# A 512-value bias row spread by TensorE, W's first block transposed after the tables, and three filler products ahead of B

## The reference, cut to what matters

```
w = weights[subjects];  b = bias[subjects]          # (128, 64, 64), (128, 64)
x = x + einsum('bct,bcd->bdt', x, w) + b[:, :, None]            # layer 0
H = einsum('btd,od->bto', x, W)                                 # W: 512 x 512
xa = einsum('btd,brd->btr', x, A[adapter_idx])                  # rank 16
delta = einsum('btr,bor->bto', xa, Bm[adapter_idx]) * scalings[adapter_idx]
x = x + H + delta                                               # layer 1
```

## Time and profile before

| | us |
|---|---|
| median of 3 runs | 241.46 |
| lowest, highest | 241.38, 241.91 |
| the profiled execution | 241.36 |
| its span | 239.6 |

### The profile page before, as it was taken

One profiled execution on the slowest core, in us unless ns is written; L12 is line 12 of the kernel. 1 busy time (PEld: TensorE's weight loads), 2 busy tenths in 40 slices (PEclk: granted clock), 3 DMA queues, 4 the chain that ended last, 5 costly groups with the idle time before them and its releaser, 6 DMA issues.

```text
span 239.6 us, 9653 instructions
## 1 busy us (share of the span) xinstructions
PE 229.4 (96%) x2900; PEld 187.7 (78%) x2901; DVE 149.2 (62%) x259; ACT 107.9 (45%) x185; POOL 79.6 (33%) x277
## 2 busy tenths in 40 slices
PE   1899999999999999999999999999999999999992
PEld 1787878888887888888888888888788888888761
DVE  6799848873358636875258835875448754425762
ACT  3184663543436363562436354454435434344441
POOL 4467771700077610610056730525135131000000
PEclk9999999999999999999999999999999999999998
DMA  5956455736565474645555574645646364562233
GB/s 132 279 169 193 141 176 156 198 94 176 148 197 141 120 213 131 201 108 192 134 154 163 147 215 109 192 115 160 172 135 191 109 200 110 155 178 63 83 78 90
DMA packets 23723, 36.64 MB, mean 153 GB/s; under 512 B 6162, under 2 KB 6162, under 8 KB 23698
## 3 DMA queue, kind: packets, MB, share of 16 engines
q1 hardware_dynamic: 16480, 26.10, 40.0%
q10 hardware_dynamic: 7218, 10.23, 13.7%
HBM read 19.53 MB, written 16.78 MB: 152 GB/s over the span
## 4 chain that ended last, share of the span: by engine, by line
PE 89%; DVE 2%; DMA 2%; ACTq 2%; issue 1%; ACT 1%; DVEq 0%
PE ps L883 69%; PE ps L843 14%; PE ps L819 3%; DMA o_ring<-in_L_cond_W_dram 2%; PE ps L764 1%; ACTq L693 1%; PE ps L775 1%; DVE o_ring L554 1%; ACT x_hi L658 1%; ACT m_f L681 1%; DVE x_lo L534 0%; PE ps L813 0%; DVE last_parts L539 0%; PE ps L871 0%; DVE o_ring L549 0%
## 5 line engine op out<-in xcount | busy, mean ns | idle before, releaser
L883 PE MATMUL ps<-m_hi,x_hi 128*128 x244 | 97.0, 398 | 0.0
L883 PE MATMUL ps<-m_hi,x_lo 128*128 x244 | 95.1, 390 | 0.0
L883 PE MATMUL ps<-m_lo,x_hi 128*128 x244 | 95.1, 390 | 0.0
L534 DVE TENSOR_TENSOR x_lo<-x,x_hi 128x512 fp32r<-128x512 f32 x64 | 44.7, 698 | 62.8 <-ACT x_hi L658 62.4
L374 POOL COPY p_pair<-p_all 64x64 f32 x128 | 42.8, 335 | 113.8 <-DVE x L526 96.9
L658 ACT ACTIVATE x_hi<-x 128x512 fp32r<-128x512 f32 x64 | 40.4, 632 | 56.0 <-ACT o_ring L671 30.9
L671 ACT ACTIVATE o_ring<-ps 128x512 f32<-128x512 f32 x60 | 35.9, 598 | 52.1 <-PE ps L883 50.7
L883 PEld LDWEIGHTS ps<-m_hi,x_hi 128*128 128x128 f32 x244 | 45.8, 188 | 10.7 <-issue 0.4
L883 PEld LDWEIGHTS ps<-m_hi,x_lo 128*128 128x128 f32 x244 | 45.8, 188 | 9.7
L883 PEld LDWEIGHTS ps<-m_lo,x_hi 128*128 128x128 f32 x244 | 45.8, 188 | 9.0
L526 DVE TENSOR_TENSOR x<-ps,bias_pair 128x512 f32<-128x512 f32 x64 | 43.6, 685 | 11.1 <-PE ps L843 10.1
(11 more groups left out here) (102 smaller groups left out, 82.4 us busy)
## 6 DMA issues: line engine op xcount, KB each, us to landing
x_ring<-in_x_dram SPq DMA_DIRECT2D x122, 128.0 KB, 2.7
out_dram<-o_ring ACTq DMA_DIRECT2D x64, 128.0 KB, 2.6
out_dram<-o_ring SPq DMA_DIRECT2D x64, 128.0 KB, 2.3
a_f<-in_L_cond_A_dram SPq DMA_DIRECT2D x8, 128.0 KB, 2.7
x_ring<-in_x_dram ACTq DMA_DIRECT2D x6, 128.0 KB, 3.4
o_ring<-in_L_cond_W_dram SPq DMA_DIRECT2D x2, 256.0 KB, 4.7
o_ring<-in_L_cond_W_dram ACTq DMA_DIRECT2D x2, 256.0 KB, 5.8
b_nat<-in_L_cond_Bm_dram ACTq DMA_DIRECT2D x1, 256.0 KB, 3.7
```

The lines of the kernel that those rows point to most:

```text
L534: nc.vector.tensor_tensor(x1_lo[:, u % HELD], x1[:, u % 2], x1_hi[:, u % HELD], ALU.subtract).then_inc(x1_lo_ready, 1)
L883: mm = nc.tensor.matmul(ps[:, 2 + u % 2, :], part, m_tile(m, k, c), start=(c == 0 and part is hi and m is m_hi), stop=(c == TC - 1 and par ...
```

## The change

1. Bias. The 256 KB DMA on ACT's queue is removed. SP loads the row to one partition (`bias_row`, 2 KB) as its second DMA, ahead of W's first block. TensorE spreads it: four products of a row of ones with 128 columns of `bias_row` each, into PSUM bank 5, three of them ahead of the order product and the fourth after the scalings. ACT copies the bank to `bias_all`.
2. W's first block is turned after the tables rather than between the scalings and the tables, and only when bank 5 is free (`bias_ready`).
3. After it stand three products of the bfloat16 identity with two copies of itself (256 columns), into the bank that B is turned into next, `keep_busy(b_bank(0), 3)`; then B is turned, and W's third block only after B.
4. x loads of the first quad: SP now loads both halves of pair 3 (five loads), ACT three.
5. `wt`: ACT copies chunks 0 to 2, DVE chunk 3, and DVE splits A before its copy.
6. POOL zeroes the second half of `a_parts` after pair 3, not at the start.
7. At the end, if pair 63 is computed apart, ACT copies its even half's lower part (`copy_last_low`) before it stores the odd item of pair 62; afterwards only the odd half's is left.

```diff
@@ block.sync
+            sp.dma_start(bias_row[:], bias.rearrange("s d -> (s d)").rearrange("(a n) -> a n", a=1)).then_inc(bias_in, 16)
             sp.dma_start(w_nat[:, 0, :], W[0:P, :]).then_inc(w_in[0], 16)
...
-            b = words(sp, regs[:5], batch[0:1, 2:7], B - 1)
+            b = words(sp, regs[:6], batch[0:1, 2:8], B - 1)
             for i in range(1, XR):
                 load_half(sp, i, 0, b[2 * i - 2], x_first[i])
+            load_half(sp, XR - 1, 1, b[2 * XR - 3], x_first[XR - 1])
             load_a(1, 1)
@@ block.gpsimd
+                if n is None and j == HEAD - 1:
+                    pool.wait_ge(pair_ready, j * 4 + 4)
+                    nc.gpsimd.memset(a_parts[0:GR, 1, :].bitcast(F32), 0.0).then_inc(rows_zeroed, 1)
+                    pool.wait_ge(rows_zeroed, 2)
@@ block.vector
-            dve.wait_ge(wt_turned, 1)
-            nc.vector.tensor_copy(wt[:, 0, :], ps[:, FIRST, :]).then_inc(wt_copied_too, 1)
             a_split(0, 0)
+            dve.wait_ge(wt_turned, TC)
+            nc.vector.tensor_copy(wt[:, TC - 1, :], ps[:, FIRST + TC - 1, :]).then_inc(wt_copied_too, 1)
@@ block.scalar
-            act.dma_start(bias_all[:], bias.rearrange("s d -> (s d)").rearrange("(a n) -> a n", a=1)
-                          .to_broadcast([P, S * C]).rearrange("p (s d) -> p s d", s=S)).then_inc(bias_in, 16)
...
-                    for half in range(2):
-                        act.wait_ge(low_done[half][i], 1)
-                        nc.scalar.activation(low[0:C, half], ps[C:2 * C, 2 + 2 * half + u % 2, :],
-                                             ACT.Copy).then_inc(low_ready, 1)
+                    for half in range(2) if j < PAIRS - 1 else (1,):
+                        copy_low_half(j, u, half)
...
+            def copy_last_low(j, u):
+                act.wait_ge(out_ready, j)
+                with act.If_ne(last_places[MIXED - 1][0], last_places[MIXED - 1][1]):
+                    copy_low_half(j, u, 0)
...
+            act.wait_ge(bias_spread, 1)
+            nc.scalar.activation(bias_all[:].rearrange("p s d -> p (s d)"), ps[:, 5, :], ACT.Copy).then_inc(bias_ready, 1)
             act.wait_ge(batches_ready, 1)
-            b = words(act, last_regs, batch[0:1, 0:2 * XR], B - 1)
-            for i in range(XR):
-                load_half(act, i, 1, b[2 * i + 1], x_first[i])
+            b = words(act, last_regs[:5], batch[0:1, 1:6], B - 1)
+            for i in range(XR - 1):
+                load_half(act, i, 1, b[2 * i], x_first[i])
...
                     copy_low(j, u)
+                    if j == PAIRS - 2:
+                        copy_last_low(j + 1, u + 1)
                     store_odd(j, u, last_batches[2 * n_of_mixed(j) + 1])
@@ block.tensor
+            def spread_bias(part):
+                cols = slice(part * P, part * P + P)
+                return nc.tensor.matmul(ps[:, 5, cols], ones[0:1, :], bias_row[:, cols], start=True, stop=True)
+            def keep_busy(bank, times):
+                for _ in range(times):
+                    nc.tensor.matmul(ps[:, bank, 0:2 * P], ident_b[:], ident_b[:].unsqueeze(1).to_broadcast([P, 2, P]),
+                                     start=True, stop=True)
+            pe.wait_ge(bias_in, 16)
+            for part in range(TC - 1):
+                spread_bias(part)
...
+            pe.wait_ge(bias_ready, 1)
+            pe.wait_ge(w_in[0], 16)
+            for c in range(TC):
+                turn_w(0, c)
+            pe.wait_ge(scal_ready, 1)
+            keep_busy(b_bank(0), 3)
+            turn_b(0)
```

More of the change, by code:

```diff
@@ L92, in cond_residual_layers @@
         scal_row = sb("scal_row", [1, K])
+        bias_row = sb("bias_row", [1, S * C])
         neg = sb("neg", [P, 2])
@@ L149, in cond_residual_layers @@
         bias_in = sem("bias_in")
+        bias_spread = sem("bias_spread")
+        bias_ready = sem("bias_ready")
         bnat_in = sem("bnat_in")
@@ L333, in _ @@
             pool.wait_ge(consts, 6)
-            for half in range(2):
-                nc.gpsimd.memset(a_parts[GR - GR * half:P - GR * half, half, :].bitcast(F32), 0.0).then_inc(rows_zeroed, 1)
-                pool.wait_ge(rows_zeroed, half + 1)
+            nc.gpsimd.memset(a_parts[GR:P, 0, :].bitcast(F32), 0.0).then_inc(rows_zeroed, 1)
+            pool.wait_ge(rows_zeroed, 1)
             pool.wait_ge(bnat_in, 16)
@@ L382, in step @@
                 if isinstance(j, int) and j == 0:
-                    pool.wait_ge(bias_in, 16)
+                    pool.wait_ge(bias_ready, 1)
                 for half in range(2):
@@ L558, in _ @@
             dve.wait_ge(zeroed, 3)
-            dve.wait_ge(rows_zeroed, 2)
+            dve.wait_ge(rows_zeroed, 1)
             dve.wait_ge(w0_in, 16)
@@ L579, in _ @@
             x1_add(2, 2)
+            dve.wait_ge(rows_zeroed, 2)
             a_split(1, 1)
@@ L671, in copy_out, with copy_low_half @@
                 nc.scalar.activation(o_ring[:, u % OR, :], ps[:, 2 + u % 2, :], ACT.Copy).then_inc(out_ready, 1)
+            def copy_low_half(j, u, half):
+                i = n_of_mixed(j)
+                act.wait_ge(low_done[half][i], 1)
+                nc.scalar.activation(low[0:C, half], ps[C:2 * C, 2 + 2 * half + u % 2, :],
+                                     ACT.Copy).then_inc(low_ready, 1)
             def copy_low(j, u):
@@ L704, in _ @@
             nc.scalar.activation(scal_all[:], ps[:, 6, 0:K], ACT.Copy).then_inc(scal_ready, 1)
+            act.wait_ge(bias_spread, 1)
+            nc.scalar.activation(bias_all[:].rearrange("p s d -> p (s d)"), ps[:, 5, :], ACT.Copy).then_inc(bias_ready, 1)
             act.wait_ge(batches_ready, 1)
-            b = words(act, last_regs, batch[0:1, 0:2 * XR], B - 1)
-            for i in range(XR):
-                load_half(act, i, 1, b[2 * i + 1], x_first[i])
+            b = words(act, last_regs[:5], batch[0:1, 1:6], B - 1)
+            for i in range(XR - 1):
+                load_half(act, i, 1, b[2 * i], x_first[i])
             a_round(0, 0)
+            copy_wt(0)
             copy_wt(1)
             copy_wt(2)
-            copy_wt(3)
             last_batches = words(act, last_regs, batch[0:1, B - 2 * MIXED:B], B - 1)
@@ L783, in _ @@
             nc.tensor.matmul(ps[:, 6, 0:K], ones[0:1, :], scal_row[:], start=True, stop=True).then_inc(scal_spread, 1)
-            pe.wait_ge(w_in[0], 16)
-            for c in range(TC):
-                turn_w(0, c)
+            spread_bias(TC - 1).then_inc(bias_spread, 1)
             pe.wait_ge(place_ready, 1)
@@ L797, in _ @@
                 turn_w(2, c)
-            turn_b(0)
             for c in range(TC):
@@ L807, in m_product_first @@
             def m_product_first(chunk):
-                if chunk == 0:
+                if chunk == TC - 1:
                     pe.wait_ge(wt_copied_too, 1)
                 else:
-                    pe.wait_ge(wt_copied, chunk)
+                    pe.wait_ge(wt_copied, chunk + 1)
                 nc.tensor.matmul(ps[:, FIRST + chunk, :], a_parts[:, 0, chunk * P:chunk * P + P], b_parts[:],
```

## The result

| | before | changed |
|---|---|---|
| median of 6 runs each, us | 241.51 (241.38 to 241.91) | 242.87 (242.30 to 243.70) |
| profiled execution, us | 241.36 | 242.30 |
| its span, us | 239.6 | 240.6 |

The ratio is 1.0045 (1.0029 to 1.0061): slower, by 1.1 us, where 1.0 faster was forecast, and outside the range.

The account below looks back on a forecast made before the run. TensorE was taken as the bound except at the start (SP's x loads for the second quad) and the end (ACT's copies, DVE's sums). 241.36 - 0.2 (start) - 0.77 (end) = 240.4 us; range 239.7 to 241.1.

Parts of the forecast that it names:

- The end: Last pairs: with one ACT copy moved ahead, pair 63's odd sum starts earlier, 0.77 us gained (bounds 0.5 to 0.86).
- Between them TensorE works through a fixed queue, so a start that is x earlier reaches the last pairs as x: Between start and end: TensorE is the bound, so any gain at the start arrives whole at the last pairs.
- B's transposes or the third block's are 110 apart rather than 213: Start, TensorE: sign expected in the profile if the clock rises early, transposes 110 ns apart.
- the 12.4 worked out for the slow pace: Start, TensorE: end of the transposes' queue in us at the old pace, against 11.93 before.
- Rival 3: Start, TensorE: clock rises no earlier than now since transposes don't count; queue ends at 12.4, time 240.7; 8%.
- All x loads may be issued 0.25 earlier: Start: the batch product, freed from W's transposes, can start at 6.47 instead of 6.72, moving x loads up 0.25 us.
- I take 3.0 and a start at 21.7: Second quad: SP's last x load lands 3.0 us after issue, not 3.6; quad starts at 21.7, 0.2 gained.
- rival 2: Start: SP's queue eats the gain, second quad starts at 22.3, 0.4 late; time 241.0; 13%.
- Each 0: Start: moving POOL's zeroing and giving `wt` to another engine each change nothing, between 0 and 0.1 us.
- Rival 5: TensorE: slower, as the clock rises early and falls again; 4%.
- The chance of 0.05 for slower: Whole kernel: probability given to the change being slower, beside 0.81 for faster and 0.14 for same.

Follow-up runs that it names:

- kernel 1: Kernel before with part 7 alone (pair 63's even copy ahead of pair 62's odd store): 240.81 us, ratio 0.996.
- kernel 3: Changed kernel plus twelve one-element products at the start of TensorE's program (about 48 instructions): 241.80 us, ratio 1.001.
- kernel 5: Changed kernel with its part 4 undone (x loads split as before): 242.51 us, ratio 1.0048.
- 9: Changed kernel with part 4 undone and twelve one-element products at the start of TensorE's program: 241.33 us, ratio 0.9989.
- 2: Kernel before plus six one-element products at the start of TensorE's program (about 24 instructions): 242.71 us, ratio 1.0039.
- 12: Kernel before plus three one-element products at the start of TensorE's program (12 instructions): 241.60 us, ratio 0.9996.
- 4: Changed kernel without part 3's three products of the identity with itself: 242.23 us, ratio 1.0019.
- 10: Changed kernel with part 4 undone, twelve one-element products at the start, and without part 3's three identity products: 241.19 us, ratio 0.9984.
- kernel 7: Kernel 1 plus four products of the identity, all 128 rows, in the gaps of TensorE's start: 240.77 us, ratio 0.9966.
- kernel 6: Kernel before with parts 4 to 7 of the change alone: 241.27 us, ratio 0.9981.
- 11: Kernel 1 plus twelve one-element products at the start of TensorE's program (48 instructions): 241.20 us, ratio 1.0002.

## Why the prediction was wrong, step by step

**The end: right.** -0.77 forecast, 0.72 in the profile, 0.86 by kernel 1's median.

**"Between them TensorE works through a fixed queue, so a start that is x earlier reaches the last pairs as x": this step failed, and it is the largest part of the miss.** Without the wait the change is still no gain: kernel 3 stands level with before (1.001, 0.9988 to 1.0032). The order of the work is fixed, but not the time at which the engine has its instructions. Parts 1 to 3 add 11 products to TensorE, and with them the place at which it stops for its next instructions came to stand early in layer 1 of pair 2. The price by medians is +1.07 (changed less 3), +1.18 (5 less 9) and +1.04 (2 less before, late x included). (Changed and 3 were timed in different sets; by their ratios the first is 0.85.) What is shown: the wait depends on the count of instructions ahead, no semaphore releases it, and it can be made and removed without touching any data. It also goes with the packet of q8 in every profile (the table above): late where the packet went out within the dense run, gone where it went out ahead of it. So 48 more instructions cost no wait: the packet then goes out 2 to 4 us sooner, while layer 1 still runs at 0.23 a product. In before it goes out late too, but the place stands later in the twelve: by the steps of kernels 2 to 12 at about the eleventh product, near 26.5 (an estimate), and 23.93 and 1.56 are 25.5. The DMA view of the changed kernel, 23.6 to 23.7, and of kernel 3, 20.6 to 20.7:

```profile
q8 instruction: 1, 0.02, 75.8%
...
q8 instruction: 1, 0.02, 92.6%
```

What is still inferred is that TensorE stands for these very instructions: no view names what a packet holds or which instruction was missing. What asks for the packet at that moment is not shown either.

**"B's transposes or the third block's are 110 apart rather than 213": failed.** The prediction let the clock rise early. In the changed kernel's profile it rose at about 12.4, and the queue of transposes ended at 12.50, which is the 12.4 worked out for the slow pace. But the early rise does come in others: of the six profiles that have the start of parts 1 to 3, four rise between 9.6 and 10.6 (4, 5, 9, 10), two at 12.1 to 12.4 (3 and changed). Kernel 7, with full products in the gaps, rises at 11.3, and none of the other seven before 11.9, the latest (6) at about 13.7. One profile of each can't say more than that an early rise came with added work only, and can't be counted on, as TensorE's program of the changed kernel alone gives 12.4 and 9.6. Rival 3 named the late rise, but for a reason (transposes don't count) that kernels 4, 5 and 10 contradict: there neighbouring transposes go from 421 ns to 273 or 274. The error cost little: where the rise was early the second quad started at 22.88 and 21.97, no sooner than before.

**"All x loads may be issued 0.25 earlier": half right; a term was put at nothing.** SP's first went out at 7.32. ACT's did not move (8.51). The copy of the bias (6.36 to 6.96) is not the reason: kernel 5 has it and issues its first x load at 8.01, kernel 6 has not and issues at 8.65. It is ACT's fetch of the batch words into registers. Part 4 has it fetch five words from the second on; before and kernel 5 fetch eight from the first on. The fetch in the changed kernel, then in 5 (min/median/max ns):

```profile
L249 ACTq TENSOR_LOAD <-batch x1: 1327/1327/1327, 6.9 to 6.9; - x1
...
L249 ACTq TENSOR_LOAD <-batch x1: 761/761/761, 6.9 to 6.9; - x1
```

It takes 1.32 in kernel 6 too, and 0.76 in before. Why fewer words take longer is not shown.

**"I take 3.0 and a start at 21.7": failed.** The start was 22.25, the number of rival 2 (22.3), but not by its path. SP's last load went out at 17.80, not 18.2, and landed at 21.73, 3.9 later. The chain has no wait ahead of 22.25: TensorE's own products ended there, with x at the same height (21.73 and 0.48 are 22.21). That rival 2's number was met is luck. I had chosen the value that needed a quicker landing than the earlier trace rows shows. The last x load of the quad lands between 20.9 and 23.3 in the profiles that show it, which varies more than the change moves it. By medians part 4 costs 0.36 (changed less 5) and 0.47 (3 less 9), and parts 4 to 6 together 0.46 (6 less 1), but by ratios changed and 5 are equal (1.0045 and 1.0048), and the intervals of the other two pairs overlap: a cost of part 4 is likely and not shown.

**POOL's zeroing moved, "Each 0": wrong where nothing else is last.** In kernels 9 and 10 POOL's copies for pairs 4 to 7 are what the quad waits for, 0.6 and 0.7 us, of which the zeroing is part; in 4 they end 0.14 after x. In the changed kernel's own profile they are on no path.

**The sum, corrected by medians:** end -0.86, place of the wait +1.1, x split +0.4, the rest of parts 1 to 3, 5 and 6 +0.1 to +0.5 (9 less 11, 9 less 1; the wait for POOL is within it): +0.7 to +1.1, against +1.2 to +1.4 measured (242.87 less 241.67 or 241.51). Some 0.3 of that is not assigned; it is as large as the scatter of the terms.

**Rival 5** (slower, as the clock falls again) did not come: the 96 products of layer 0 from 14.33 took 1.56, as in the earlier trace rows (1.60). The chance of 0.05 for slower held only mishaps with data and clock, none with instructions.

The best version is the end alone: kernel 1 at 0.996, and kernel 7 equal to it.

## What to carry to other kernels

Cut a change that has a sure gain at one end from the parts that rearrange the other: here the copy moved at the end is worth 0.86 us alone, and with the six parts around the start the kernel is 2.06 above that (242.87 less 240.81). When an engine is the bound and its program grows, even by 20 instructions at an idle moment, look in the profile after for a wait of "issue" without a releaser just behind its densest run; adding or removing a few instructions far ahead tells at once whether it is bound to a place in the program, and the DMA view shows when the packets of kind "instruction" go out and come in. And where a wait for a load stands at the same height as the engine's queue, take the duration that the row shows, not a better one.

## What was not expected of the hardware

- A wait of 0.74 to 1.20 us on TensorE that moves with its program: 24 instructions more made it (241.67 to 242.71), 48 more removed it (242.87 to 241.80). It ends 1.28 to 1.56 after a 16 KB packet of kind "instruction" has landed.
- ACT's fetch of five batch words, from the second on, took 1.33 us; that of eight, from the first on, 0.76.
- TensorE's clock rose to 2.4 GHz at 12.4 us in one run and at 9.6 in another (5) with the same program on TensorE.
- The same x load landed 3.6, 4.24 and 5.18 us after its issue, and with it the second quad started between 21.9 and 23.8.
